# A fused attention and time-mix kernel on one core: where two pieces of the key/value projection, the query projection and one set of mixing products stand between the score tiles

## The chip, the core and the metric

One core of a Trainium2 chip runs the whole program. The metric is device time in microseconds of one execution. The kernel before was timed three times: 1163.57, 1166.56 and 1168.26 us, so its median is 1166.56 us.

## The reference

The input is x (8 batch elements of 256 rows, 256 channels) and a context of 8 x 1601 x 256. Layer 0 is cross attention with 32 query heads and 8 key/value heads of width 8; layer 1 is an RWKV block whose state has 32 heads of 8 x 8.

```
q = x @ Wq + bq;  k = ctx @ Wk + bk;  v = ctx @ Wv + bv
attn = softmax(q k^T * scale + mask);  x = LN((attn v) @ Wo + bo + x) * gamma + beta
xa = ln(x);  sx = previous row of xa - xa
xxx = tanh((xa + sx * maa_x) @ maa_w1), in five parts, each @ maa_w2[f]
xk, xw, xv, xr, xg = xa + sx * (maa_stack + xxx)
w = exp(-exp(time_decay + tanh(xw @ td_w1) @ td_w2));  r, k, v from xr, xk, xv;  g = silu(xg @ Wg^T)
for each row: out = r (u * k v^T + s);  s = k v^T + w * s
og = groupnorm(out) * g;  x1 = x + og @ Wo^T
rr = sigmoid(xr2 @ Wfr^T);  out = x1 + rr * (relu(xk2 @ Wfk^T)^2 @ Wfv^T)
```

## The kernel before

The work is a software pipeline over the 8 batch elements. In turn `it` (0 to 9) five elements are in work at once (`elements`): b is `it` and has its attention scores, exponentials and weighted sums computed; a is `it + 1` and has its values turned and its row maxima found; f is `it + 2` and has its keys, values and queries projected; c is `it - 1` and runs the attention output product, the mixing and the state recurrence; d is `it - 2` and ends its feed-forward part. Turns 1 to 5 have all of a, b, c and f; turn 0 has no c; turns 6 and 7 have b and c and no f; turns 8 and 9 have no b and drain the pipeline.

A turn has 52 steps (4 groups of heads by 13 chunks of 128 context rows). Each step has two score tiles, 0 and 1 (`score_tile`: two bf16 matmuls each into `ps[0]` or `ps[1]`). ScalarE takes the exponential of each tile (`exp_tile`, 128 x 1024 elements), and TensorE uses the result in `weigh` (8 fp32 matmuls per step). A score tile may be written only when the exponential two tiles earlier is done, since there are two score buffers; `weigh` waits for both exponentials of its step. Everything else that TensorE does is written out by hand between those: `side(step, ...)` at even steps, `score_rows` at any step. What `side` does for a step comes after both tiles of the next step. The order of TensorE's score and weigh work is chosen by two tables: in a LIGHT step one `weigh` stands between the tiles of a step and one between those of the next; in other steps both stand together after the tiles of the even step; in a DIVIDED step (14 and 40) one stands before the tiles of the next step and one after `side`.

What the change touches:

- `project_kv(f, n, bank)` projects one of four pieces of the keys and values (4 fp32 matmuls of 400 columns). Pieces 0 to 3 stand at steps 30, 32, 40 and 42 (`KV_STEP`) and write banks 5, 5, 6, 7. VectorE adds the bias (`bias_kv`) and GpSimd waits for all four and splits the keys into bf16 parts (`split_k_high`, `split_k_mid`, `split_k_low`).
- `project_q(f, 7)` projects the queries at step 46 (8 fp32 matmuls of 256 columns, two halves m) into bank 7; VectorE scales them in `scale_q(f, 7)`, which stands after the row moments of x1 and ahead of the scaled rows xn.
- `mixes(c, [(2, 5), (1, 7)])` at step 14 multiplies two parts of the tanh output by maa_w2 (8 matmuls of 256 columns). It waits for `h_ready`, two tanh that ScalarE does after the exponentials of step 14.
- On ScalarE, step 40 also holds a square root (`std_o`), which needs its table loaded, and then the exponential's table again.
- On VectorE the chain from the square root to `og` (reciprocal, product, gn scale and bias, product with the gate) ends in what TensorE's Wo product at step 44 waits for; `bias_kv(f, 3)` stands behind that chain.
- SyncE issues the load of the next mask at step 44, after waiting for all four pieces of f, since it overwrites `ctx_t`.

The kernel keeps a second, general pass behind a flag that these inputs do not raise; the same tables serve it.

Of the kernel before, what the change touches and what calls it, by code (L numbers as in the profile page):

```python
# [13 lines left out]
EC, LC = E // P, L // P  # L14
NC = -(-S // P)
# [33 lines left out]


DIVIDED = (NC + 1, 3 * NC + 1)
LIGHT = (2, 4, 8, 10, 12, 20, 24, 26, 28, 38, 48, 50)


KV_FIRST = (0, 1, 2, 3)
KV_SECOND = (5, 6, 5, 6)
KV_BANK = (5, 5, 6, 7)
KV_STEP = [30, 32, 40, 42]
A_ROUND, B_ROUND = 33, 10

FILLERS = {10: 24, 12: 7, 16: 6, 36: 2, 38: 3, 44: 20, 48: 11, 50: 8}
# [38 lines left out]
def build(nc, dram, out):  # L100
    ctx = ExitStack()
    with ctx:
# [120 lines left out]
        kv_proj, kv_biased = sig("kv_proj", NK), sig("kv_biased", NK)  # L223
# [604 lines left out]
        def _(pe):  # L828
# [7 lines left out]
                    last = mm(bank(to)[:, 0:w], w_kv[:, e, :], ctx_t[:, e, at:at + w], e == 0, e == EC - 1)  # L836
                last.then_inc(kv_proj.sem, 1)

            def project_q(a, to):
                pe.wait_ge(xt_in.sem, xt_in.at(a))  # L840
                for m in range(EC):
                    for e in range(EC):
                        last = mm(halves(to)[:, m, :], w_q[:, e, P * m:P * m + P], x_t[:, e, :], e == 0, e == EC - 1)
                    last.then_inc(q_proj.sem, 1)
# [142 lines left out]
            def side(step, it, lo, general):  # L987
# [6 lines left out]
                if c is not None:  # L994
# [6 lines left out]
                    elif step == 10:  # L1001
                        pe.wait_ge(xn_ready.sem, xn_ready.at(c))
                        turn_rows(xn, 5, xt_turned)
                    elif step == 12:
                        pe.wait_ge(mix_ready.sem, mix_ready.at(c))
                        for e in range(EC):
                            mm(halves(5)[:, 0, :], w1[:, e, 0:P], mix[:, e, :], e == 0, e == EC - 1)
                        for e in range(EC):
                            last = mm(halves(5)[0:32, 1, :], w1[:, e, P:160], mix[:, e, :], e == 0, e == EC - 1)
                        last.then_inc(h_done.sem, 2)  # L1010
                    elif step == 16:
                        pe.wait_ge(xm_ready.sem, xm_ready.at(c, 1))
                        if b is not None:
                            pe.wait_ge(shift_kept[1].sem, shift_kept[1].at(b))
                        elif d is not None:
                            pe.wait_ge(ff_used.sem, ff_used.at(d))
                        product(wsq["Wv"], xm[2], 6, v_done)
                        pe.wait_ge(xm_ready.sem, xm_ready.at(c, 2))
                        for e in range(EC):
                            last = mm(bank(7)[0:64, 0:L], td1[:, e, :], xm[1][:, e, :], e == 0, e == EC - 1)  # L1020
                        last.then_inc(td1_done.sem, 1)
                    elif step == 18:
                        pe.wait_ge(td1_ready.sem, td1_ready.at(c))
                        mixes(c, [(0, 5), (3, 7)])
                    elif step == 20:
                        pe.wait_ge(xm_ready.sem, xm_ready.at(c, 3))
                        product(wsq["Wk"], xm[0], 5, k_done)
                    elif step == 22:
                        pe.wait_ge(xxx_used.sem, xxx_used.at(c, 4))
                        for m in range(EC):  # L1030
                            last = mm(halves(7)[:, m, :], w2_last[:, P * m:P * m + P], h_b[:, :])
                        last.then_inc(xxx_done.sem, 1)
                    elif step == 24:
                        pe.wait_ge(xm_ready.sem, xm_ready.at(c, 4))
                        pe.wait_ge(w_log_ready.sem, w_log_ready.at(c))
                        product(wsq["Wr"], xm[3], 6, r_done)
                    elif step == 26:
                        pe.wait_ge(xm_ready.sem, xm_ready.at(c, 5))
                        product(wsq["Wg"], xm[4], 7, g_done, (0,))
                    elif step == 28:  # L1040
                        product(wsq["Wg"], xm[4], 7, g_done, (1,))
                    elif step == 34:
                        if f is not None:
                            pe.wait_ge(kv_biased.sem, kv_biased.at(f, 2))
                        else:
                            pe.wait_ge(k_ready.sem, k_ready.at(c))
                        gather(c, 0)
                        gather(c, 1)
                    elif step == 38:
                        pe.wait_ge(d_squared.sem, d_squared.at(c))  # L1050
                        mm(bank(5), block[:, :, :], d_sq[:, :, :]).then_inc(o_var.sem, 1)
                    elif step == 44:
                        pe.wait_ge(og_ready.sem, og_ready.at(c))
                        if f is not None:
                            pe.wait_ge(kv_biased.sem, kv_biased.at(f, 3))
                        elif a is not None:
                            pe.wait_ge(shift_kept[0].sem, shift_kept[0].at(a))
                        else:
                            pe.wait_ge(bonus_ready.sem, bonus_ready.at(c))
                        product_rows(og, wsq["Wo"], 6, x1_done)  # L1060
                    elif step == 48:
                        pe.wait_ge(xn2_ready.sem, xn2_ready.at(c))
                        if f is not None:
                            pe.wait_ge(q_scaled.sem, q_scaled.at(f))
                        turn_rows(xn, 7, xt2_turned)
                    elif step == 50:
                        pe.wait_ge(xr2_ready.sem, xr2_ready.at(c))
                        pe.wait_ge(x1_ready.sem, x1_ready.at(c))
                        product_rows(xr2, wsq["Wfr"], 6, rr_done)
# [54 lines left out]
                if f is not None:  # L1124
                    for n in range(NK):
                        if step != KV_STEP[n]:
                            continue
                        if n == 0:
                            if c is not None:
                                pe.wait_ge(k_ready.sem, k_ready.at(c))  # L1130
                            else:
                                pe.wait_ge(v_kept.sem, v_kept.at(a))
                        elif n == 1:
                            pe.wait_ge(kv_biased.sem, kv_biased.at(f, 1))
                        elif n == 2:
                            pe.wait_ge(shift_kept[0].sem, shift_kept[0].at(a))
                        elif c is not None:
                            pe.wait_ge(d_ready.sem, d_ready.at(c))
                        else:
                            pe.wait_ge(sub_reduced[0].sem, sub_reduced[0].at(a))  # L1140
                        project_kv(f, n, KV_BANK[n])
                    if step == 46:
                        pe.wait_ge(kv_biased.sem, kv_biased.at(f))
                        project_q(f, 7)

            def first_projection(a, general):
                for n in range(NK):
# [18 lines left out]
            def all_turns(lo, general):  # L1166
                first_projection(lo, general)
                for it in range(lo, lo + B + 2):
                    f, a, b, c, d = elements(it, lo)
                    for step in range(0, STEPS, 2):  # L1170
# [15 lines left out]
                        if b is not None:  # L1186
                            score_tile(b, step + 1, 0, general)
                            if light:
                                weigh(b, step - 1)
                            score_tile(b, step + 1, 1, general)  # L1190
                        score_rows(step, it, lo, general)
                        side(step, it, lo, general)
                        if b is not None and step in DIVIDED:
                            weigh(b, step - 1)
                        if it == B and step == 26 and not general:
# [14 lines left out]
        def _(dve):  # L1210
# [15 lines left out]
            def bias_kv(f, n, at_bank):  # L1226
                at, w = PIECE[n]
                dve.wait_ge(kv_proj.sem, kv_proj.at(f, n + 1))
                if n == 0:
                    dve.wait_ge(v_turned.sem, v_turned.at(f - 1))  # L1230
                    dve.wait_ge(k_low.sem, k_low.at(f - 1))
                nc.vector.tensor_scalar(kv32[:, at:at + w], bank(at_bank)[:, 0:w], b_kv[:, 0:1], None, ALU.add)\  # L1232
                  .then_inc(kv_biased.sem, 1)
# [176 lines left out]
            def all_turns(lo, general):  # L1410
# [28 lines left out]
                for it in range(lo, lo + B + 2):  # L1439
# [117 lines left out]
                        keep_output(b, 2)  # L1557
                    if f is not None:
                        bias_kv(f, 2, KV_BANK[2])
                    if c is not None:  # L1560
                        dve.wait_ge(d_ready.sem, d_ready.at(c))
                        dve.wait_ge(std_ready.sem, std_ready.at(c))
# [2 lines left out]
                        for e in range(EC):  # L1565
# [2 lines left out]
                        link(last)  # L1568
                        nc.vector.scalar_tensor_tensor(og[:, :, :], d_c[:, :, :], 0.5, g_c[:, :, :], ALU.mult, ALU.mult)\
                          .then_inc(og_ready.sem, 1)  # L1570
                    if f is not None:
                        bias_kv(f, 3, KV_BANK[3])
                    if c is not None:
                        if it == B and not general:
                            raise_flag()
# [2 lines left out]
                        dve.wait_ge(x1_ready.sem, x1_ready.at(c))  # L1578
                        row_moments(x1, c, 2)
                    if f is not None:  # L1580
                        scale_q(f, 7)
                    if c is not None:
                        scaled_rows(xn, x1, c, 2).then_inc(xn2_ready.sem, 1)
                        dve.wait_ge(xt2_turned.sem, xt2_turned.at(c))
# [71 lines left out]
```

## Time and profile before

| | |
|---|---|
| median of three runs | 1166.56 us |
| the profiled execution | 1166.92 us |
| its span, first to last instruction | 1165.1 us |
| granted TensorE clock, mean over the span | 0.950 |
| PE busy | 1043.2 us (90%) |
| ACT busy | 860.1 us (74%) |
| DVE busy | 590.2 us (51%) |
| POOL busy | 323.1 us (28%) |
| DMA | 91.65 MB, mean 79 GB/s |

PE is TensorE, ACT is ScalarE, DVE is VectorE, POOL is GpSimd. The first exponential of turn 1 starts at 166.88 us, of turn 2 at 291.80, of turn 3 at 417.74, of turn 6 at 797.18, of turn 7 at 923.64; the last exponential ends at 1048.78 us, and the 116.3 us after it are the drain. In the timeline a row merges equal neighbours: its first number is the start, the second the time from the first start to the last end, and `x8` the count. A row's end overlaps the next row's start a little, since matmuls are pipelined. 64x512 bf16 rows are score tiles (x2 is one tile), `probs,v_aug` rows are `weigh` (x8 is one step).

### The profile page before, as it was taken

Reading aid. Unit: us, or ns where it says so; the run is one execution under the profiler, and the core shown is the slowest. Engines: PE = TensorE matmul, PEld = TensorE weight load, DVE = VectorE, ACT = ScalarE, POOL = GpSimd, SP = SyncE. Lnnn points to the kernel's source line nnn. Section 1 sums busy time; section 2 is a strip of 40 time slices with the busy share of each in tenths; the row PEclk is TensorE's granted clock in tenths of the full one; section 3 lists DMA queues with packets and bytes.
Section 4 is the critical chain, followed back from the end, with each engine's and each line's share of the span. In section 5 each row is a group of like instructions: output and inputs, shape, how many; then the busy total and the mean of one; then the engine's idle time right before and its main releaser. Section 6 shows DMA issues by size and latency. Waiting matters only on the chain.

```text
span 1165.1 us, 17951 instructions
## 1 busy us (share of the span) xinstructions
PE 1043.2 (90%) x7021; PEld 355.6 (31%) x7021; DVE 590.2 (51%) x951; ACT 860.1 (74%) x940; POOL 323.1 (28%) x363
## 2 busy tenths in 40 slices
PE   4298989999999999999999999999998899877876
PEld 2031223323333233323332333323331333223413
DVE  5040117555647365754745564836574364445554
ACT  2178888888888888888888888888888888880110
POOL 3670061232214141415024231414141002400330
PEclk8599999999999999999999999999999999998667
DMA  4945024722445233802472254523260035000400
GB/s 137 219 130 146 14 74 106 140 45 71 118 66 119 72 76 66 162 7 78 109 132 53 71 118 61 125 73 73 66 100 16 15 93 78 5 14 14 72 1 12
DMA packets 68876, 91.65 MB, mean 79 GB/s; under 512 B 9664, under 2 KB 49648, under 8 KB 68784
## 3 DMA queue, kind: packets, MB, share of 16 engines
q1 hardware_dynamic: 64608, 85.25, 33.1%
q0 software_dynamic: 2480, 4.12, 1.8%
q10 hardware_dynamic: 1696, 1.06, 0.4%
q8 instruction: 57, 0.93, 0.3%
q14 instruction: 35, 0.29, 0.1%
HBM read 50.74 MB, written 18.62 MB: 60 GB/s over the span
## 4 chain that ended last, share of the span: by engine, by line
PE 56%; ACT 17%; issue 15%; DVE 6%; POOL 3%; DMA 2%; ACTq 1%; SPq 0%; POOLq 0%; DVEq 0%
PE psum L830 55%; ACT probs L769 13%; DVE vs L1366 1%; POOL xm L605 1%; DMA ctx_t<-in_mask 1%; POOL vs L628 1%; ACT L769 1%; ACT L801 1%; POOL vs L619 1%; ACTq L295 1%; DMA q_stack<-q_stacked 1%; PE psum L920 1%; ACT xm L798 0%; ACT xm L801 0%; PE psum L851 0%
## 5 line engine op out<-in xcount | busy, mean ns | idle before, releaser
L769 ACT ACTIVATE probs<-psum 128x1024 f32<-128x1024 f32 (+1 forms) x832 | 798.6, 1022 | 184.6 <-PE psum L830 182.1
L830 PE MATMUL psum<-probs,v_aug 128*9 128x512 f32 (+1 forms) x3328 | 425.9, 603 | 1.3 <-DVE o_raw L1308 1.2
L830 PE MATMUL psum<-q_stack,k_stack 64*128 64x512 bf16 (+1 forms) x1745 | 324.4, 393 | 59.6 <-ACT probs L769 45.5
L830 PEld LDWEIGHTS psum<-q_stack,k_stack 64*128 64x128 bf16 (+1 forms) x1745 | 84.5, 95 | 478.4 <-ACT probs L769 384.4
L1373 DVE TENSOR_TENSOR_SCAN vs<-w_c,vs 128x514 f32<-128x514 f32 x64 | 102.6, 1604 | 21.3 <-POOL vs L619 19.4
L628 POOL TENSOR_TENSOR vs<-r_c,vs 128x512 f32<-128x512 f32 x64 | 86.6, 1363 | 87.0 <-DVE tmp L1523 49.7
L605 POOL TENSOR_TENSOR xm<-tmp,xa 128x512 f32<-128x512 f32 x40 | 46.0, 1167 | 232.3 <-DVE tmp L1360 232.3
L830 PEld LDWEIGHTS psum<-probs,v_aug 128*9 128x9 f32 (+1 forms) x3328 | 58.4, 89 | 149.4 <-issue 141.2
L1308 DVE COPY o_raw<-psum 128x512 f32<-128x512 f32 x32 | 22.1, 691 | 111.8 <-PE psum L830 111.8
L592 POOL TENSOR_TENSOR rstd<-moments,eps 128x2 f32<-128x2 f32 x24 | 4.7, 196 | 239.7 <-DVE moments L1326 239.7
L1360 DVE SCALAR_TENSOR_TENSOR tmp<-psum,chan,sx 128x256 f32<-128x256 f32 x80 | 33.5, 477 | 61.6 <-PE psum L830 61.6
L830 PE MATMUL psum<-ctx_t,w_kv 128*128 128x400 f32 (+1 forms) x128 | 53.3, 547 | 5.8 <-DMA ctx_t<-in_ctx_t 5.2
L1366 DVE TENSOR_TENSOR vs<-k_c,vs 128x512 f32<-128x512 f32 x64 | 54.5, 851 | 0.3
L564 POOL CAST k_parts<-kv 64x1601 bf16<-64x1601 f32 x7 | 10.6, 1520 | 157.0 <-DVE kv L1232 157.0
L1232 DVE TENSOR_SCALAR kv<-psum,b_kv 128x400 f32<-128x400 f32 (+1 forms) x28 | 17.5, 626 | 60.8 <-PE psum L830 60.8
L830 PEld LDWEIGHTS psum<-ctx_t,w_kv 128*128 128x128 f32 x128 | 23.4, 200 | 27.0 <-issue 14.5
L1563 DVE RECIPROCAL xm<-xm 128x512 f32<-128x512 f32 x8 | 26.8, 3347 | 7.1 <-ACT xm L801 7.1
L1255 DVE TENSOR_REDUCE row_max<-psum 128x16 f32<-128x512 f32 x32 | 20.5, 682 | 19.4 <-PE psum L830 19.4
L1249 DVE TENSOR_REDUCE mask_max<-ctx_t 128x1 f32<-128x1601 f32 x16 | 28.8, 1811 | 0.5 <-DMA ctx_t<-in_mask 0.5
L1313 DVE RECIPROCAL den_t<-den_t 128x512 f32<-128x512 f32 x8 | 26.8, 3345 | 3.3 <-DMA den_t<-o_raw 3.3
L830 PE MATMUL psum<-k_stack,q_stack 48*128 48x32 bf16 x512 | 9.0, 174 | 21.3 <-DMA q_stack<-q_stacked 21.3
L1577 DVE TENSOR_TENSOR x<-psum,x 128x512 f32<-128x512 f32 x8 | 5.5, 692 | 44.4 <-PE psum L830 44.4
(177 smaller groups left out, 1033.3 us busy)
## 6 DMA issues: line engine op xcount, KB each, us to landing
vs<-v_c SPq DMA_DIRECT2D x61, 257.0 KB, 7.3
ctx_t<-in_mask SPq DMA_DIRECT2D x8, 1601.0 KB, 6.8
k_stacked<-k_parts SPq DMA_DIRECT2D x48, 200.1 KB
ctx_t<-in_ctx_t SPq DMA_DIRECT2D x24, 400.0 KB, 6.3
k_stack<-k_stacked SPq DMA_DIRECT2D x31, 300.2 KB, 6.5
q_stack<-q_stacked SPq DMA_DIRECT2D x31, 192.0 KB, 6.8
q_stacked<-q_parts SPq DMA_DIRECT2D x88, 64.0 KB, 3.3
ctx_t<-in_ctx_t SPq DMA_DIRECT2D x8, 401.0 KB, 6.4
```

The costliest lines, as they stand in the source:

```text
L605: nc.gpsimd.tensor_tensor(xm[MIX_ORDER[n]][:, :, :], tmp[n % 2][:, :, :], xa[:, :, 1:L + 1], ALU.add)\
L628: nc.gpsimd.tensor_tensor(vs[:, j, :, 0:L], r_c[:, :, :], vs[:, j, :, 0:L], ALU.mult)\
L769: nc.scalar.activation(probs[turn_step % NP][t][0:w, :, :], ps[t][0:w, :, :], ACT.Exp).then_inc(exped.sem, 1)
L830: return nc.tensor.matmul(dst, lhsT, rhs, start=start, stop=stop)
L1249: nc.vector.tensor_reduce(mask_max[:, a, lc:lc + 1], ctx_t[:, lc, :], AX.X, ALU.max, apply_absolute_value=True).then_inc(mask_seen.sem, 1)
L1255: last = nc.vector.tensor_reduce(row_max[:, :].rearrange("p (r a u) -> p r a u", a=2, u=4)[:, :, half, :], bank(6 + half).rearrange("p (r ...
L1308: nc.vector.tensor_copy(o_raw[:, :], po).then_inc(o_kept.sem, 1)
L1313: nc.vector.reciprocal(den_t[:, :, :], den_t[:, :, :]).then_inc(den_turned.sem, 1)
L1360: last = nc.vector.scalar_tensor_tensor(tmp[n % 2][:, e, :], halves(at)[:, e, :], vec(f"s{f}", e), sx[:, e, :], ALU.add, ALU.mult)
L1366: nc.vector.tensor_tensor(vs[:, j, :, 1:L + 1], k_c[:, :, :], vs[:, j, :, 1:L + 1], ALU.mult)\
L1373: nc.vector.tensor_tensor_scan(flat, w_c[:, :, :].rearrange("p e l -> p (e l)"), flat, 0.0, ALU.mult, ALU.add)\
L1563: link(nc.vector.reciprocal(std_o[:, :, :], std_o[:, :, :]))
```

## The change

Piece 3 of the keys and values moves from step 42 to step 40, right behind piece 2. The query projection is split into its two halves: the first goes to step 42 and the second stays at step 46; both write bank 5 instead of bank 7. Step 42 becomes LIGHT. The products of step 14 move from behind tile 1 of step 15 to between its two tiles (`INNER`). On VectorE the bias of piece 3 moves ahead of the group-norm chain, and `scale_q` reads bank 5. Two waits change with the banks: step 42 waits for the square root that read bank 5, and the turning of xn at step 48 waits for piece 3's bias where it waited for the scaled queries.

```
-LIGHT = (2, 4, 8, 10, 12, 20, 24, 26, 28, 38, 48, 50)
+LIGHT = (2, 4, 8, 10, 12, 20, 24, 26, 28, 38, 42, 48, 50)
+INNER = (NC + 1,)
-KV_STEP = [30, 32, 40, 42]
+KV_STEP = [30, 32, 40, 40]

-            def project_q(a, to):
+            def project_q(a, to, parts=range(EC)):
                 pe.wait_ge(xt_in.sem, xt_in.at(a))
-                for m in range(EC):
+                for m in parts:

                     elif step == 48:
                         pe.wait_ge(xn2_ready.sem, xn2_ready.at(c))
                         if f is not None:
-                            pe.wait_ge(q_scaled.sem, q_scaled.at(f))
+                            pe.wait_ge(kv_biased.sem, kv_biased.at(f))

-                    if step == 46:
-                        pe.wait_ge(kv_biased.sem, kv_biased.at(f))
-                        project_q(f, 7)
+                    if step == 42:
+                        if c is not None:
+                            pe.wait_ge(std_ready.sem, std_ready.at(c))
+                        else:
+                            pe.wait_ge(kv_biased.sem, kv_biased.at(f, 2))
+                        project_q(f, 5, (0,))
+                    elif step == 46:
+                        project_q(f, 5, (1,))

                             score_tile(b, step + 1, 0, general)
                             if light:
                                 weigh(b, step - 1)
+                            if step in INNER:
+                                side(step, it, lo, general)
                             score_tile(b, step + 1, 1, general)
                         score_rows(step, it, lo, general)
-                        side(step, it, lo, general)
+                        if b is None or step not in INNER:
+                            side(step, it, lo, general)

                     if f is not None:
                         bias_kv(f, 2, KV_BANK[2])
+                        bias_kv(f, 3, KV_BANK[3])
...
-                    if f is not None:
-                        bias_kv(f, 3, KV_BANK[3])
...
-                        scale_q(f, 7)
+                        scale_q(f, 5)
```

## Rows read from the trace of the kernel before

**Rows 1.** Windows of turns 2, 3, 6: length, busy us, then clock, DMA share, GB/s.
```profile
291.80:417.74 125.94, 121.94 (x869) 42.10 (x867) 72.04 (x117) 106.67 (x117) 36.20 (x37) 1.00 0.40 87
417.74:545.31 127.57, 123.57 (x869) 42.21 (x867) 72.05 (x117) 106.67 (x116) 36.19 (x37) 0.99 0.39 86
797.18:923.64 126.46, 115.65 (x845) 38.11 (x843) 67.96 (x111) 106.24 (x116) 28.28 (x31) 0.99 0.32 59
```
**Rows 2.** Timeline of PE, turn 2, steps 14 to 15.
```profile
326.03 0.39 PE L830 MATMUL psum<-q_stack,k_stack 64*128 64x512 bf16 x2 [0.53 <-ACT probs L769]
326.54 1.13 PE L830 MATMUL psum<-h_a,w 32*128 32x256 f32 x8
327.60 1.04 PE L830 MATMUL psum<-probs,v_aug 128*9 128x512 f32 x8
```
**Rows 3.** Timeline of ACT in the same stretch.
```profile
326.13 0.36 ACT L781 ACTIVATE h_b<-psum 32x256 f32<-32x256 f32 x1
326.39 1.91 ACT L769 ACTIVATE probs<-psum 128x1024 f32<-128x1024 f32 x2
329.07 1.94 ACT L769 ACTIVATE probs<-psum 128x1024 f32<-128x1024 f32 x2 [0.77 <-PE psum L830]
```
**Rows 4.** Timeline of PE, turn 2, step 40 to the next turn.
```profile
389.09 1.61 PE L830 MATMUL psum<-ctx_t,w_kv 128*128 128x400 f32 x4
390.63 1.04 PE L830 MATMUL psum<-probs,v_aug 128*9 128x512 f32 x8
393.10 0.39 PE L830 MATMUL psum<-q_stack,k_stack 64*128 64x512 bf16 x2 [1.43 <-ACT probs L769]
394.02 0.39 PE L830 MATMUL psum<-q_stack,k_stack 64*128 64x512 bf16 x2 [0.52 <-ACT probs L769]
...
396.71 1.61 PE L830 MATMUL psum<-ctx_t,w_kv 128*128 128x400 f32 x4
398.26 0.80 PE L830 MATMUL psum<-q_stack,k_stack 64*128 64x512 bf16 x4
...
406.19 1.99 PE L830 MATMUL psum<-x_t,w_q 128*128 128x256 f32 x8
...
411.31 0.66 PE L920 MATMUL psum<-ident,xn 128*128 128x128 f32 x4
...
413.20 0.88 PE L830 MATMUL psum<-q_stack,k_stack 64*128 64x512 bf16 x4
...
417.25 0.61 PE L830 MATMUL psum<-q_stack,k_stack 64*128 64x512 bf16 x4
```
**Rows 5.** Timeline of ACT, turn 2, steps 41 to 44.
```profile
392.02 3.77 ACT L769 ACTIVATE probs<-psum 128x1024 f32<-128x1024 f32 x4
396.67 4.02 ACT L769 ACTIVATE probs<-psum 128x1024 f32<-128x1024 f32 x4 [0.87 <-PE psum L830]
```
**Rows 6.** Timeline of DVE, turn 2; the last row is from turn 3.
```profile
391.29 3.35 DVE L1563 RECIPROCAL xm<-xm 128x512 f32<-128x512 f32 x1
...
396.17 0.69 DVE L1569 SCALAR_TENSOR_TENSOR xm<-xm,g_c 128x512 f32<-128x512 f32 x1
...
409.08 2.06 DVE L1333 TENSOR_SCALAR xn<-x,moments,rstd 128x256 f32<-128x256 f32 x2
...
440.08 0.74 DVE L1333 TENSOR_SCALAR xn<-x,moments,rstd 128x256 f32<-128x256 f32 x2 [1.16 <-POOL rstd L595]
```
**Rows 7.** Timeline of POOL, turn 2.
```profile
406.17 3.23 POOL L568 TENSOR_TENSOR k_rest<-kv,k_parts 64x1601 f32<-64x1601 f32 x1
409.47 1.51 POOL L570 CAST k_parts<-k_rest 64x1601 bf16<-64x1601 f32 x1
```
**Rows 8.** Timeline of PE at step 42: turn 3, then turn 6.
```profile
520.49 3.33 PE L830 MATMUL psum<-probs,v_aug 128*9 128x512 f32 x16
...
898.47 0.39 PE L830 MATMUL psum<-q_stack,k_stack 64*128 64x512 bf16 x2 [2.84 <-ACT probs L769]
...
899.93 3.06 PE L830 MATMUL psum<-probs,v_aug 128*9 128x512 f32 x16
```

## The prediction

> **What bounds the kernel now.** I read the windows of the turns first, then the waits of each engine, then the timelines of the stretches that the diff touches. In turn 2, with all five elements in work, TensorE is busy 121.94 of 125.94 us and ScalarE 106.67; turn 3 is the same but for 1.63 us more at a lower clock [rows 1]. So TensorE is nearly always the bound: ScalarE idles before its next pair of exponentials because a matmul group came between (0.77 us at step 16, 0.87 at step 43 [rows 3, 5]). The exception is where ScalarE waits on nothing but itself: the square root and two table loads of step 40 hold its exponentials of step 41 back to 392.02, and TensorE stands 1.43 us and then 0.52 [rows 4, 5]. That hole is what the change fills. The turns with all elements repeat to 0.01 us but for the clock, so I replay turn 2 and multiply.
>
> **Prices for the replay**, each from a row of turn 2, where a group's end overlaps the next start by about 0.07: a tile alone 0.32 (0.39 less 0.07), a pair of tiles 0.54 (0.61 less 0.07), one weigh 0.98 (1.04 less 0.07, rounded up), a KV piece 1.54 (389.09 to 390.63), half the query projection 0.96 (half of 1.99 less 0.07) [rows 4]; the step-14 products 1.06 (326.54 to 327.60) [rows 2]. Exponentials follow each other by 0.92 and take 1.02; a tile starts 0.06 after the exponential that frees its buffer (392.02 + 1.02 + 0.06 = 393.10), and its exponential can start 0.49 after it (tiles at 396.71 - 0.54 = 396.18, exponential 396.67) [rows 4, 5].
>
> **Steps 40 to 44, turns 1 to 5.** The third piece runs 389.09 to 390.63 as now, the fourth behind it to 392.17 (its data and bank 7 are free by then), weigh 39 to 393.15. Step 42's tile 0 was at 393.10, so the whole piece costs 0.05: 1.43 us of idle and no more hid it. Step 42 is now LIGHT: weigh 40 to 394.45 covers the wait of 0.52 for tile 1; tile 1 at 394.45; step 43's tile 0 needs exponential 42.0, which starts at 393.86 at the earliest and ends at 394.88, so 394.94; weigh 41 from 395.26 to 396.24; tile 1 to 396.56; the query half to 397.52. Step 44's tile 0 is there at 397.52, tile 1 waits for exponential 43.1 (396.78 + 1.02), so 397.86, and the step's weighs start at 398.18. Before, they started at 398.26 + 0.72 = 398.98. Gain so far 0.80. The parts: the piece leaves step 42 (1.54), the half comes in (0.96), and the other 0.22 comes from the weighs that LIGHT puts into tile waits.
>
> **Step 46.** The other half takes 0.96 where 1.93 stood, so 0.80 becomes 1.76; but step 48's tile 0 now meets exponential 47.0 and starts 0.08 late: 1.69. Step 49's tile 0 meets exponential 48.0 and starts 0.23 late. TensorE then reaches the turning of xn at 409.90 instead of 411.31.
>
> **Step 48: the next late thing.** xn2 is made by two VectorE instructions at 409.08 that take 2.06 us, where the same two take 0.74 in a free stretch [rows 6]. They stand while GpSimd splits the keys: its subtract ends at 409.40, its cast runs 409.47 to 410.98 [rows 7], and xn2 ends at 411.14, just in time for 411.31. In the new kernel GpSimd's split hangs on x1 as before (it comes after the root of x1's variance), and x1 moves by only 0.80 with the Wo product. The scaled queries come 1.7 us earlier, so VectorE starts xn2 at about 407.25, still inside the subtract (405.37 to 408.60) and then the cast (to 410.18): xn2 ends at 410.34, and the turning starts at 410.40. The gain is 0.91 there. A wait of 0.22 for exponential 50.0 at step 51 (0.81 from 413.20 to the next group, where a pair needs 0.59) mostly goes, since ScalarE has caught up [rows 4]: step 0 of the next turn comes at 416.11 instead of 417.25. **Gain 1.14 per turn, 5.7 for five.** The Trainium skill ("SBUF — State Buffer", Who interferes with whom) says that VectorE in a two-port mode and GpSimd hold one pair of ports in turn and the second to come stands for the whole instruction. The trace agrees: 2.06 against 0.74. If the subtract and cast did not block, the turn would gain 1.62.
>
> **VectorE and the queues.** The bias of piece 3 (0.64) now stands before the reciprocal and waits for the piece, so the chain starts 1.54 later: og at 396.86 + 1.54 = 398.40. The Wo product, now at 400.56, needs it: 2.16 of slack, which hides the step; if GpSimd's first cast (1.5 us, now as early as 393) delays the chain by its own length, 0.6 is left. So this costs 0 while that slack holds, and everything beyond 2.16 would count in full. The mask load on SyncE's queue starts some 6 us earlier beside the attention rows, whose consumer is at the end of the turn: 0. The new waits (square root at 390.72, fourth bias) are over long before TensorE comes: 0.
>
> **Turn 0** has no c: the fourth piece adds 1.54 at step 40, leaves 1.54 at step 42, where 0.96 comes in, and 0.96 leaves at step 46. ScalarE runs without square root there, so nothing hides the move, and its two shifts cancel: 0, within 0.6 either way.
>
> **Turns 6 and 7** have no f; there only LIGHT acts. At step 42 TensorE stands 2.84 us and then for tile 1 [rows 8]. Replayed as above at full clock, step 44's weighs start at 903.47 instead of 904.36: 0.88 each, **1.8**.
>
> **Step 14, turns 1 to 7.** Both tanh must be done before the products: h_b ends at 326.49 and the products start at 326.54 [rows 2, 3]. Tile 1 of step 15 (326.03 to 326.35) now lies inside that wait and costs nothing. Moved behind the products it cannot make them earlier: products 326.54 to 327.60, tile 1 to 327.92, weigh 13, step 16 at 328.90 instead of 328.58. Exponential 15.1 starts at 328.09 instead of about 327.30 and ends at 329.11; exponential 16.0 starts at 329.39 instead of 329.07, so ScalarE's 0.77 of idle takes in the later 15.1. **Cost 0.32 in each of seven turns, 2.2.** Bounds: 0 (if step 16 met another wait, but the row behind shows none) and 0.79, the full delay of 15.1, if ScalarE's idle were not there.
>
> **The clock.** Three times in turns 1 to 7 the granted clock fell to 1.2 GHz, each time behind these waits of step 42: turn 3 (16 matmuls in 3.33 us where 1.90 is usual, 1.63 for the turn), turn 6 (3.06) and turn 7 [rows 1, 8]. In turns 1 to 5 the wait is gone, so the fall of turn 3 goes: **1.6**. In turns 6 and 7 2.84 of idle stays; I leave those falls as they are, with up to 1.4 each as luck.
>
> **Sum**, against the profiled execution (span 1165.10, 1.82 around it, 1166.92 in all; 0.36 over the median): -5.7 - 1.8 - 1.6 + 2.2 = -6.9, so 1160.0. The drain keeps its work; where its clock falls is luck, some 2 us either way, about the spread of the three runs.
>
> **Rivals.**
> A. xn2 isn't held by GpSimd (VectorE gets through first), and the falls of turns 6 and 7 go as well: 5 x 0.48 + 1.4 = 3.8 more, 1156. For it: 1.7 us more of room ahead of the cast. Against it: the subtract holds the first of the two instructions already.
> B. Step 14 costs the full 0.79, with 7 x 0.47 = 3.3 more: 1163.5, within 0.5%. For it: ScalarE's second tile comes after the products in every turn. Against it: the 0.77 of idle behind.
> C. Slower: the new wait at step 15, from the first tile's end (326.03 - 0.53 = 325.50) to 326.54 without a break, 1.04 us, brings the clock down as step 42's did. At turn 3's price of 1.63 in seven turns that is 11.4: 1171.4. It decides from the fifth such turn on (6.9 / 1.63 = 4.2). Against it: 1.43 and 0.52 together brought the clock down in one turn of five, and 1.04 is less. The Trainium skill ("TensorE: Matmul & The Clock Gate", A second HAM failure mode) says that small idles between matmul groups can make the clock swing; the trace shows it for step 42 alone.
> D. The fourth piece is not hidden, since VectorE's og comes over 2.2 us late: the 0.80 of step 44 goes, five times, 1164.
>
> **Chances.** Forecast 0.50, A 0.22, B and D 0.22, C 0.06. Range 1155.5 to 1165.5. The measurement tells 0.5% (5.8 us, so 1160.7) from no change; my number lies just past it: faster 0.58, same 0.36, slower 0.06.
>
> **What would show it.** In turn 2: no idle over 0.2 at step 42, step 42's tile 0 within 0.1 of where it was relative to step 40; the exponential 15.1 some 0.8 later and step 16 0.32 later; og before the Wo product; a wait of about 0.5 on xn at step 48; the turn 0.8 shorter (125.1), turn 6 0.6 shorter. It is wrong if turns 1 to 5 shrink by less than 0.5 each, if TensorE waits for og, or if the clock falls near step 15.

## The result and the profile after

The changed kernel took 1170.14 us (median of 11 runs, 1164.29 to 1174.53), the kernel before 1165.77 (11 runs, 1163.57 to 1169.02): ratio 1.0037, 95% interval 1.0024 to 1.0049. It is slower by 4 us, where 1160.0, some 6 us faster, was forecast. The profiled execution of the changed kernel is one of its faster ones: 1166.98 us, span 1165.2 against 1165.1.

The turns say where the time went. The first exponentials of turns 0 to 7 stand at 50.63, 163.40, 287.49, 412.59, 539.22, 666.04, 794.31 and 921.68, and the last ends at 1050.17. Windows of turns 2, 3, 5 and 6 of the changed kernel, columns as in [rows 1]:

```profile
287.49:412.59 125.10, 121.98 (x869) 42.24 (x867) 72.90 (x117) 106.74 (x116) 36.16 (x37) 1.00 0.41 88
412.59:539.22 126.63, 123.51 (x869) 42.09 (x867) 72.91 (x117) 106.73 (x116) 36.15 (x37) 0.99 0.40 87
666.04:794.31 128.27, 125.15 (x869) 42.52 (x867) 72.91 (x117) 106.73 (x117) 36.17 (x37) 0.97 0.39 86
794.31:921.68 127.37, 117.31 (x845) 37.92 (x843) 67.95 (x111) 106.48 (x117) 28.47 (x31) 0.97 0.32 58
```

Turn 2 is 125.10 long, where 125.94 stood [rows 1] and 125.12 was worked out. But turns 4 to 7 are longer than before by up to 3.4 us, and turn 3, 0.94 shorter than before, is longer than turn 2; the clock of turns 3 to 7 is lower. A stretch in which the granted clock is at half is called a fall below. The next fence has windows of the changed kernel behind step 15: turn 2, then turns 3, 4, 5, 6, 7. The granted clock (third number from the end) is full in the first and half, the level of 1.2 GHz, in the others:

```profile
323.00:327.00 4.00, 4.00 (x36) 0.79 (x32) 1.66 (x4) 3.02 (x4) 2.14 (x2) 1.00 0.14 31
448.50:451.90 3.40, 3.40 (x18) 0.39 (x20) 1.66 (x4) 1.48 (x2) 2.14 (x2) 0.50 0.17 39
574.90:578.20 3.30, 3.30 (x16) 0.36 (x14) 1.66 (x4) 1.02 (x1) 1.89 (x2) 0.51 0.14 32
701.10:707.80 6.70, 6.70 (x34) 1.50 (x34) 1.66 (x4) 3.49 (x4) 2.14 (x2) 0.50 0.11 23
830.90:834.10 3.20, 3.20 (x20) 0.42 (x16) 0.98 (x3) 2.06 (x3) 2.14 (x2) 0.50 0.18 38
957.10:963.80 6.70, 6.70 (x34) 1.50 (x34) 1.66 (x4) 3.49 (x4) 2.14 (x2) 0.50 0.12 23
```

What goes ahead of each is the same. TensorE's timeline, changed kernel, turn 2 and then turn 5; it answers to [rows 2]:

```profile
320.80 0.39 PE L831 MATMUL psum<-q_stack,k_stack 64*128 64x512 bf16 x2
322.23 1.13 PE L831 MATMUL psum<-h_a,w 32*128 32x256 f32 x8 [1.03 <-ACT h_b L782]
323.29 0.39 PE L831 MATMUL psum<-q_stack,k_stack 64*128 64x512 bf16 x2
...
700.77 1.85 PE L831 MATMUL psum<-h_a,w 32*128 32x256 f32 x8 [1.03 <-ACT h_b L782]
702.56 0.61 PE L831 MATMUL psum<-q_stack,k_stack 64*128 64x512 bf16 x2
703.10 1.89 PE L831 MATMUL psum<-probs,v_aug 128*9 128x512 f32 x8
```

TensorE idles 1.03 us before the products, as replayed (1.04). In turn 5 the clock falls while they run: they take 1.85 instead of 1.13, and weigh 13 1.89 instead of 1.05. In the profiled executions, from before to after, turns 1, 2, 3 give -0.82, -0.83, -0.94, turns 4 to 7 +0.89, +2.34, +0.91, +3.36, the drain -1.3, the start -0.75, together about 0. Turn 0 gives -2.7: one fall of the kernel before (89.9 us, at its step 15) is missing from this execution, though the wait ahead of it, 1.21 us, is there in both, and the low clock of the start ends 5.3 us behind the first exponential instead of 7.8. That is luck, and the medians show what is left without it. Two falls at step 42 of turns 6 and 7 stand in both executions; that of turn 7 is twice as long here.

Steps 40 to 48 of turn 2 of the changed kernel, on TensorE; they answer to [rows 4]:

```profile
385.10 2.95 PE L831 MATMUL psum<-ctx_t,w_kv 128*128 128x400 f32 x8
387.99 1.05 PE L831 MATMUL psum<-probs,v_aug 128*9 128x512 f32 x8
389.12 0.39 PE L831 MATMUL psum<-q_stack,k_stack 64*128 64x512 bf16 x2
...
392.57 1.13 PE L831 MATMUL psum<-x_t,w_q 128*128 128x256 f32 x4
...
396.54 1.99 PE L831 MATMUL psum<-w_Wo,xm 128*128 128x256 f32 x8
...
403.73 0.89 PE L831 MATMUL psum<-q_stack,k_stack 64*128 64x512 bf16 x4
...
406.37 0.66 PE L921 MATMUL psum<-ident,xn 128*128 128x128 f32 x4 [0.44 <-DVE xn L1342]
...
412.10 0.60 PE L831 MATMUL psum<-q_stack,k_stack 64*128 64x512 bf16 x4
```

The hole of 1.43 is gone: step 42's tile 0 starts 0.15 after weigh 39 can be over (387.99 + 0.98 = 388.97). The two pieces took 2.89 (385.10 to 387.99), less than twice the 1.54 of one, so there was that much to spare. From step 41's tiles (384.26) to the next turn's step 0 (412.10) are 27.84 us; before they were 29.00 (388.25 to 417.25), so 1.16 less. And TensorE stands 0.44 for xn2, as forecast.

### The profile page after: what moved, and what is told of

It reads as the page before. It is cut to its first block, busy times and chain, and to the rows that moved or that the text cites. A ratio compares the mean times of both kernels' runs of the same rounds, so it can differ in the third digit from the quotient of the medians.

```text
span 1165.2 us, 17951 instructions
## 1 busy us (share of the span) xinstructions
PE 1048.4 (90%) x7021; PEld 355.4 (30%) x7021; DVE 594.5 (51%) x951; ACT 860.7 (74%) x940; POOL 323.0 (28%) x363
## 4 chain that ended last, share of the span: by engine, by line
PE 54%; issue 16%; ACT 15%; DVE 8%; POOL 3%; DMA 2%; ACTq 1%; SPq 0%; DVEq 0%; POOLq 0%
PE psum L831 53%; ACT probs L770 12%; DVE xn L1342 1%; DVE vs L1375 1%; POOL xm L606 1%; DMA ctx_t<-in_mask 1%; PE psum L921 1%; POOL vs L629 1%; ACT L770 1%; ACT L802 1%; POOL vs L620 1%; ACTq L296 1%; DMA q_stack<-q_stacked 1%; ACT xm L799 0%; ACT xm L802 0%
## 5 line engine op out<-in xcount | busy, mean ns | idle before, releaser
L831 PE MATMUL psum<-probs,v_aug 128*9 128x512 f32 (+1 forms) x3328 | 430.3, 607 | 1.3 <-DVE o_raw L1317 1.2
L831 PE MATMUL psum<-ctx_t,w_kv 128*128 128x400 f32 (+1 forms) x128 | 50.0, 528 | 5.9 <-DMA ctx_t<-in_ctx_t 5.3
L1342 DVE TENSOR_SCALAR xn<-x,moments,rstd 128x256 f32<-128x256 f32 x32 | 23.6, 778 | 12.7 <-POOL rstd L596 12.7
L1509 DVE COPY v_c<-psum 128x512 f32<-128x512 f32 x8 | 5.5, 693 | 44.9 <-PE psum L831 44.9
```

The lines of the kernel that those rows point to most:

```text
L831: return nc.tensor.matmul(dst, lhsT, rhs, start=start, stop=stop)
L1342: last = nc.vector.tensor_scalar(dst[:, t, :], x[:, t, :], moments[:, t, 0:1], rstd[:, t:t + 1], ALU.subtract, ALU.mult)
```

## The experiments

Three theories. **Theory 1**: the idle of 1.04 us at step 15 brings TensorE's clock down (rival C of the prediction). **Theory 2**: the gain at steps 40 to 48 isn't real over many executions. **Theory 3 (order)**: what costs is that the products stand between the tiles. Each kernel was timed in turns with the kernel before, in three groups in which the median of the kernel before was 1166.0, 1165.25 and 1166.21. Ratios are to that median, with a 95% interval. Medians stand on 4 to 12 runs, and one execution of each kernel was profiled.

**no_inner**: the change without its part at step 15.

```
-INNER = (NC + 1,)
+INNER = ()
```

> The changed kernel with the products of step 14 back behind both tiles of step 15, all else kept. Theory 1 (the idle of 1.04 us at step 15 lowers TensorE's clock): the low clock near step 15 is gone in all turns, turns 1 to 5 last 124.8 us (turn 2: 125.94 before, 1.14 less), and the time is 1166 - 5.7 - 1.8 - 1.6 = 1157 us, ratio to before 0.992. Theory 2 (the parts at steps 40 to 48 bring nothing outside this profile, or are lost again in the drain): 1165 to 1168, ratio 1.000.

1159.93 us (1153.75 to 1165.80), ratio 0.9949 (0.9931 to 0.9967). Turn 2 is 124.79. Over turns 1 to 7 the clock falls only at step 42 of turns 6 and 7; the first window is all of them (two falls of 3.4 us in 873 still round to 1.00), the others stand behind step 15 of turns 2 and 3:

```profile
166.60:1039.40 872.80, 836.95 (x5954) 282.35 (x5955) 494.81 (x792) 744.78 (x812) 232.43 (x245) 1.00 0.37 78
326.00:330.00 4.00, 4.00 (x36) 0.77 (x32) 1.66 (x4) 2.83 (x3) 2.14 (x2) 1.00 0.14 31
451.00:455.00 4.00, 4.00 (x35) 0.88 (x34) 1.66 (x4) 2.79 (x4) 2.13 (x2) 1.00 0.16 35
```

Theory 2 falls. The rest of the change is worth 6 us; its profiled execution (1156.07) is at the replay's 1157, the median 3 over it.

**inner_only**: the kernel before with that part alone.

```
+INNER = (NC + 1,)
...
                                 weigh(b, step - 1)
+                            if step in INNER:
+                                side(step, it, lo, general)
                             score_tile(b, step + 1, 1, general)
...
-                        side(step, it, lo, general)
+                        if b is None or step not in INNER:
+                            side(step, it, lo, general)
```

> The kernel before with only the products of step 14 moved between the tiles of step 15. Theory 1 (clock): 0.32 in seven turns and a fall of the clock in most of them at 1.5 to 3.2 us each, as in the changed kernel: 1166 + 2.2 + 8 to 14 = 1176 to 1182, with low clock near step 15. Theory 3 (the order alone costs: 0.32 in seven turns, and the falls in the changed kernel come from what precedes in that kernel): 1168, ratio 1.002, no low clock near step 15.

1175.07 us, ratio 1.0092 (1.0070 to 1.0114). Windows behind step 15 of turns 1, 2, 3 and 7:

```profile
200.80:204.00 3.20, 3.20 (x16) 0.26 (x12) 1.31 (x4) 1.79 (x2) 2.13 (x2) 0.50 0.17 37
330.50:333.70 3.20, 3.20 (x20) 0.37 (x16) 1.10 (x3) 1.97 (x3) 2.13 (x2) 0.50 0.16 35
460.20:463.40 3.20, 3.20 (x20) 0.42 (x16) 0.90 (x3) 2.17 (x3) 2.13 (x2) 0.50 0.20 42
968.80:972.00 3.20, 3.20 (x18) 0.33 (x20) 1.39 (x4) 1.75 (x2) 2.14 (x2) 0.50 0.19 38
```

The falls need nothing else of the change. A turn without a fall (turns 4 and 5) is 126.26, 0.33 over 125.93: the order's own price. 9 us is a little under the expectation; four of seven turns fell at step 15 in this execution. Not all of the 9 us lies there. Turns 1, 2 and 3 fell a second time, at step 42, whose waits of 1.43 and 0.53 this kernel shares with the kernel before, which of turns 1 to 5 fell there in turn 3 alone. In turn 2:

```profile
398.70:402.00 3.30, 3.30 (x18) 0.47 (x12) 2.18 (x5) 1.23 (x2) 0.00 (x0) 0.50 0.00 0
```

Turns 1 and 2, with two falls each, are 3.6 us longer than in the kernel before, and turn 7, with one more fall than there, 1.8. Whether the fall at step 15 brings on the one at step 42 isn't shown.

**wait_first**: idle kept, order put back.

```
                             score_tile(b, step + 1, 0, general)
...
+                            if step == NC + 1 and c is not None:
+                                pe.wait_ge(h_ready.sem, h_ready.at(c))
                             score_tile(b, step + 1, 1, general)
```

> The changed kernel with the products behind both tiles again, but tile 1 of step 15 waits for the two tanh of step 14, as the products do. TensorE's idle is 1.04 us as in the changed kernel, and the products no longer stand between the tiles. Theory 1 (idle lowers the clock): low clock near step 15 in most turns, 1168 to 1172, the changed kernel's time within 3 us. Rival (the products between the tiles, with the second exponential 0.8 late, are what costs): 1157 + 2.2 = 1159, no low clock there.

1168.47 us, ratio 1.0018 (1.0005 to 1.0032), within 3 us of the changed kernel and 8.5 over no_inner, from which it differs by this wait alone. TensorE before the tile in turn 2, and the clock behind it in turns 1, 2 and 3 (turn 6 fell too):

```profile
326.31 0.39 PE L831 MATMUL psum<-q_stack,k_stack 64*128 64x512 bf16 x2 [1.04 <-ACT h_b L782]
```
```profile
201.10:204.30 3.20, 3.20 (x16) 0.31 (x20) 1.66 (x4) 1.04 (x2) 2.14 (x2) 0.50 0.18 38
327.40:330.60 3.20, 3.20 (x16) 0.26 (x12) 1.66 (x4) 0.70 (x2) 1.51 (x2) 0.50 0.17 33
453.70:460.30 6.60, 6.60 (x32) 1.39 (x32) 1.66 (x4) 3.01 (x4) 2.13 (x2) 0.50 0.12 25
```

So theory 3 falls: with the products behind both tiles the clock falls all the same. A turn without a fall (turn 5) is 125.11, 0.31 over no_inner, so about 2.2 of the 8.5 us are the wait itself and some 6 the clock.

**inner_filled** and **inner_filled2**: order kept, idle filled.

```
                             if step in INNER:
+                                if c is not None:
+                                    pe.wait_ge(sub_reduced[1].sem, sub_reduced[1].at(b))
+                                    for n in range(4):    # range(2) in inner_filled2
+                                        mm(halves(7)[:, 0, :], w_kv[:, n % 2, :], w_q[:, n % 2, :])
                                 side(step, it, lo, general)
```

> The changed kernel, order kept, with four extra fp32 matmuls of 256 columns (0.96 us in all) in the idle between tile 0 of step 15 and the products; they write a half of bank 7 that the products then overwrite. Theory 1: idle about 0.1, no low clock near step 15, and only the 0.32 per turn stays: 1157 + 2.2 = 1159, ratio 0.994. Rival (order): as the changed kernel, 1170, or more by what the extra matmuls take.

1162.48 us, ratio 0.9973 (0.9957 to 0.9989). The count was a mistake: each fp32 call shows as two matmuls, so the four took 1.92 us, ran over the idle and made turn 2 125.91. Even so the kernel is 8 us faster than the changed one, with 7 x 0.8 more time in its turns, and no turn of its profiled execution fell at step 15.

> As inner_filled, with half of the extra matmuls (0.96 us as measured; the run before took 1.92 and ran over the idle by 0.8 us a turn). Theory 1: no low clock near step 15 and turn 2 of 125.1, so no_inner's time plus 7 x 0.32 = 1162. Rival: falls come back since 0.1 of idle stays at each side, 1166 or more.

1156.06 us, ratio 0.9922 (0.9901 to 0.9943). Turn 2 is 125.10, as in the changed kernel, and turns 3, 4, 5 are 125.10, 125.26, 125.10. Its step 15, and windows over that step in turns 3 and 5:

```profile
324.52 0.39 PE L831 MATMUL psum<-q_stack,k_stack 64*128 64x512 bf16 x2
324.84 1.13 PE L831 MATMUL psum<-w_q,w_kv 128*128 128x256 f32 x4
325.94 1.13 PE L831 MATMUL psum<-h_a,w 32*128 32x256 f32 x8
```
```profile
446.00:454.00 8.00, 8.00 (x54) 3.20 (x57) 5.71 (x13) 5.67 (x9) 0.82 (x1) 1.00 0.03 8
697.00:705.00 8.00, 8.00 (x56) 2.91 (x58) 5.11 (x11) 5.67 (x8) 1.46 (x2) 1.00 0.06 11
```

Matmuls whose result nobody reads make the changed kernel 14 us faster. It was expected at 1162 from no_inner plus 2.2, and is 4 below no_inner itself. One reading is that the wait of 0.53, which no_inner keeps at step 15, costs it clock in some executions; the profiled execution of no_inner (1156.07) has no fall there, so it doesn't show this. Theory 1 stands: with the idle kept, in either order, the clock falls at step 15 (four or five turns of seven), and with the order kept and the idle filled it does not.

**no_inner_fill15** tests that: no_inner with one such call between the tiles of step 15.

```
+                            if step == NC + 1:
+                                pe.wait_ge(sub_reduced[1].sem, sub_reduced[1].at(b))
+                                mm(halves(7)[:, 0, :], w_kv[:, 0, :], w_q[:, 0, :])
                             score_tile(b, step + 1, 1, general)
```

> no_inner with one extra matmul pair of 256 columns (0.48 us) in the wait of 0.53 us before tile 1 of step 15, into the half of bank 7 that the products overwrite; no order or wait changes. Theory 1 (no_inner still loses to the clock at step 15 in some executions, which is why its median of 1159.9 lies over the replay's 1157): turn 2 stays at 124.8 and the median falls to 1156 to 1157.5, with less spread. Rival (the 3 us are of the drain or the start): 1159 to 1160.

1154.54 us, ratio 0.9897 (0.9870 to 0.9924), turn 2 124.77. The median went as expected and further, but the six runs spread from 1148.38 to 1159.08, so the spread did not shrink as expected, and the reading stays open. The profiles speak for neither side: turns 1 to 7 together last 873.9 us here and 872.8 in no_inner (both without a fall at step 15, and here with one near step 35 of turn 6), and the shorter time comes from turn 0, 112.79 against 115.36. The call stands in turn 0 too, where the fall at step 15 is missing; but it was missing in the changed kernel as well, which has no such call.

**no_light**: no_inner without 42 in LIGHT.

```
-LIGHT = (2, 4, 8, 10, 12, 20, 24, 26, 28, 38, 42, 48, 50)
+LIGHT = (2, 4, 8, 10, 12, 20, 24, 26, 28, 38, 48, 50)
```

> no_inner without step 42 among the LIGHT steps. By the replay: the weighs of step 42 stand together again, 0.22 in five turns and 0.88 in turns 6 and 7 come back, 2.9 us over no_inner. Rival (LIGHT's share is nil, the piece and the query half bring everything): no_inner's time within 0.5.

1161.45 us, ratio 0.9968 (0.9953 to 0.9984): 1.5 over no_inner, between the two expectations and inside the scatter of both kernels. In the profiles its turns without a fall (3 and 5) are 125.59 and 125.60 against 124.80, so LIGHT is worth 0.80 in such a turn where 0.22 was worked out, and the piece and the query half without it 0.34 (125.93 less 125.59) where 0.92 was; the medians don't settle its sum. Two turns here (2 and 4) fell at step 15 with the old wait of 0.53.

**mid_early**: no_inner, with GpSimd's subtract and cast behind og and ahead of the root.

```
                     if f is not None:
                         split_k_high(f)
+                        if c is not None:
+                            pool.wait_ge(og_ready.sem, og_ready.at(c))
+                        split_k_mid(f)
                     if c is not None:
                         root(c, 2)
                     if f is not None:
-                        split_k_mid(f)
```

> The kernel no_inner with GpSimd's subtract and cast of the keys (split_k_mid) moved ahead of the root of x1's variance, behind og; nothing of GpSimd then stands beside VectorE's xn2 at step 48. Theory (GpSimd's instructions hold xn2 back, which makes TensorE wait at step 48): xn2's two instructions take 0.74 us instead of 2.06, the wait of 0.5 goes, turns 1 to 5 last 0.48 less than in no_inner (turn 2: 124.3), 2.4 in all. Rival (TensorE waits there for other reasons): turn 2 stays at 124.8.

1153.84 us, ratio 0.9903 (0.9881 to 0.9925). VectorE's xn2 in the changed kernel, and here, both turn 2:

```profile
403.39 2.92 DVE L1342 TENSOR_SCALAR xn<-x,moments,rstd 128x256 f32<-128x256 f32 x2
```
```profile
405.06 0.73 DVE L1344 TENSOR_SCALAR xn<-x,moments,rstd 128x256 f32<-128x256 f32 x2
```

The wait for xn2 is gone, and turns 3 and 5 last 124.26 against 124.80: 0.54 each. In the changed kernel the two instructions end at 406.31, 0.15 behind GpSimd's cast (404.65 + 1.51 = 406.16). That fits what the Trainium skill ("SBUF — State Buffer", Who interferes with whom) says of the shared ports, that the engine which comes second stands for the whole instruction of the first; the size is this trace's. The medians differ by 6.1, more than 5 x 0.54 = 2.7; the rest isn't explained. Turn 2 of this execution fell at step 15, with the old wait of 0.53.

**early_fill67**: mid_early, with two calls of 512 columns in the hole at step 42 of turns 6 and 7.

```
+                if step == 40 and f is None and b is not None and c is not None:
+                    pe.wait_ge(d_ready.sem, d_ready.at(c))
+                    for n in range(2):
+                        mm(bank(7), w_kv[:, n, :], w_q[:, :, :])
```

> mid_early with 2 us of extra fp32 matmuls in the idle of 2.84 us at step 42 of turns 6 and 7, where no key/value piece stands; they write bank 7, which nothing reads before step 48 overwrites it. Theory 1 (idle lowers the clock): no fall near step 42 in turns 6 and 7, each about 1.2 us shorter, 2.4 in all against mid_early. Rival (the fall comes by other causes there): falls stay, same time as mid_early.

1148.56 us (four runs), ratio 0.9856 (0.9833 to 0.9880), 5.3 under mid_early, twice the expectation. mid_early's hole in turn 6, and the same place here:

```profile
888.00 0.61 PE L833 MATMUL psum<-q_stack,k_stack 64*128 64x512 bf16 x2 [2.84 <-ACT probs L772]
888.53 1.89 PE L833 MATMUL psum<-probs,v_aug 128*9 128x512 f32 x8
```
```profile
888.12 0.39 PE L833 MATMUL psum<-q_stack,k_stack 64*128 64x512 bf16 x2 [1.05 <-ACT probs L772]
888.44 1.05 PE L833 MATMUL psum<-probs,v_aug 128*9 128x512 f32 x8
```

Between 51 us and the end of turn 7 its clock falls once, in turn 0. mid_early fell in turn 6, for twice the usual length, and not in turn 7. Turn 6 is 2.2 us shorter now (124.18 against 126.39) and turn 7 0.66 (122.47 against 123.13), where a wait of 0.59 us for xn near step 12 is gone. That makes 2.9 us; the other 2.4 between the medians are not explained.

**best_fill15** (early_fill67 with the call of no_inner_fill15) and **best_w13** (early_fill67 with weigh 13 in that place).

```
+                            if step == NC + 1:
+                                weigh(b, step - 1)
                             score_tile(b, step + 1, 1, general)
...
-                        if b is not None and step in DIVIDED:
+                        if b is not None and step in DIVIDED and step != NC + 1:
                             weigh(b, step - 1)
```

> early_fill67 with the same extra matmul pair at step 15. By theory 1 it guards against falls there: 1148 or a little under, turns as in early_fill67. Rival: the extra matmuls delay tile 1, turns 0.1 to 0.3 longer, 1149 to 1150.

1151.49 us, ratio 0.9882 (0.9867 to 0.9897); turns 1 to 7 are those of early_fill67 to 0.01. There was no fall left to prevent in turns 1 to 7; a longer start (52.31 us to the first exponential, against 51.14) and drain (116.0 against 113.8), less 0.95 in turn 0, carry the difference of the profiled executions, and what moves them wasn't looked into.

> early_fill67 with weigh 13 moved from behind the products to between the tiles of step 15, so that useful work stands in that wait. Weigh 13 waits until VectorE has copied the first group's sum (about 0.5 after tile 0 ends), so by the replay step 16 comes 0.27 earlier in seven turns, the idle stays at 0.5: 1148.5 - 1.9 = 1146.7. Rival: exponential 15.1 comes later and takes the gain back, or the clock falls at step 15, 1149 to 1152.

1148.57 us, ratio 0.9865 (0.9848 to 0.9883). Turns are 0.19 shorter (124.08 against 124.27), not 0.27, which the medians can't tell. These two, early_fill67 and best_w13, are 1.4% faster than the kernel before and 1.8% faster than the changed one.

## Why the prediction was wrong

Wrong in sign, by one term: the clock at step 15, which the sum put at nothing. Of the 10 us between 1160.0 and 1170.14, some 8 are that term (1170.14 less no_inner's 1159.93 less 7 x 0.31), and the other 2 are what no_inner, with these 2.2, lies over the forecast. Point by point:

- **Steps 40 to 48**: 1.14 per turn was forecast. no_inner's turn 2 is 124.79 against 125.94, 1.15. Right, the wait on xn2 among it (0.50 forecast, 0.44 found), though GpSimd was worth 0.54 a turn and not 0.48. The total came out and its shares did not: LIGHT was put at 0.22 and is worth 0.80. Rival A is out: xn2 is held, and the falls of turns 6 and 7 stay.
- **Turns 6 and 7**: 0.88 each was forecast; no_inner and the kernel before, each with one fall of the same length at step 42, differ by 0.99 and 0.94. Right. **Turn 0** was put at 0, and differs by 0.14 between these two.
- **Step 15's order**: 0.32 forecast; 0.33 in inner_only, 0.31 between the changed kernel and no_inner. Right. Rival B is out (its sum, 1160.0 + 3.3, is 1163.3 and not 1163.5).
- **VectorE's chain**: og came at 394.21 (393.52 + 0.69, the row below), the Wo product at 396.54, 2.3 of slack. Rival D is out.

```profile
393.52 0.69 DVE L1579 SCALAR_TENSOR_TENSOR xm<-xm,g_c 128x512 f32<-128x512 f32 x1
```

- **The clock**: this step failed. The forecast took one gain (the fall of turn 3, 1.6) and charged nothing for the new idle of 1.04 us, and rival C, which priced exactly this at 1.63 a turn and named the fifth turn as the point of decision, got 0.06. It happened in five of seven turns of the profiled execution, and two of the falls lasted twice as long: against no_inner, turns 3, 4, 5, 6, 7 are longer by 1.83, 1.85, 3.47, 1.90 and 4.30, which less 0.31 each (and 1 to 2 of luck at step 42 of turn 7) is some 10 us in these two executions, and 8 by the medians. Rival C's 1171.4 is near the result in part by luck, since it had seven falls of 1.63. The argument against it was "1.43 and 0.52 together brought the clock down in one turn of five, and 1.04 is less". That compared two idles by their length, from one execution. Why the shorter one is followed by falls more often stays open; what runs round them may matter, and no run tells. The trace had a warning: in turn 0 of the kernel before a wait of 1.21 us at step 15 had already been followed by 1.2 GHz, as the row and the window below show, and the prediction counted falls in turns 1 to 7 only.

```profile
89.49 1.51 PE L830 MATMUL psum<-probs,v_aug 128*9 128x512 f32 x8 [1.21 <-DVE o_raw L1308]
```
```profile
90.00:93.20 3.20, 3.20 (x18) 0.23 (x10) 0.00 (x0) 1.02 (x1) 0.00 (x0) 0.50 0.51 176
```

- **The gain from falls that go**: the fall of turn 3 at step 42 is gone as forecast. But in which turns falls come differs between executions, so one profile is a poor count of them. no_inner's 3 us over the replay may lie there too; it was not shown.

## What to carry to other kernels

When an order moves work behind a wait, price the wait twice: what it delays, and the clock. For the second, look at every place where the trace shows a fall, and at the stretch before the moved wait, not at the longest idle that did no harm. Where TensorE must wait, try useful or even useless matmuls there, and measure over ten runs: a replay was right to 0.02 us per turn while some 8 us hung on the clock.

## What the runs showed of the hardware

- In the profiled executions an idle of 1.03 to 1.04 us on TensorE at step 15, which is otherwise busy there (from 690.00 to 699.70 us of the changed kernel without a gap), was followed by 3.2 to 6.7 us at 1.2 GHz in five of seven turns of the changed kernel, four of inner_only and four of wait_first. With 0.53 us at the same place it was three turns in six kernels' 42 (two in no_light, one in mid_early). With the idle filled it was none in 14 (inner_filled, inner_filled2).
- 1.43 and 0.52 us of idle at step 42 of turns 1 to 5 were followed by a fall in one of five turns of the kernel before and in three of five of inner_only. The 2.84 us at step 42 of turns 6 and 7 were followed by one, or it began within them, in 18 of 20 turns of ten kernels; with 2 us of matmuls in them, in none of 6.
- The Trainium skill ("TensorE: Matmul & The Clock Gate", A second HAM failure mode) speaks of small idles between groups of matmuls that make the clock swing. These counts agree and give a size; they don't give a length of idle that is safe.
- The extra fp32 matmuls, whose results nobody reads, went with a clock of 2.4 GHz at the places they filled in turns 1 to 7. What makes an idle of the same length end in a fall in one turn and not in the next isn't shown.
- VectorE's two instructions on SBUF rows took 2.92 us beside GpSimd's subtract and cast in the changed kernel, and 0.73 with GpSimd idle in mid_early; the scaling of the queries, which reads PSUM, took 0.87 to 0.88 in both cases.
